# Statistics between eight stages from products and table guesses, and expert results scattered inside the loop

## The reference

```python
x = x + _layernorm(_L0_attn_ref(_layernorm(x, axis=-1), ...), axis=-1)
...
x = x + _layernorm(_L3_ffn_ref(_layernorm(x, axis=-1), ...), axis=-1)
```

## Time and profile before

| | |
|---|---|
| median of 3 runs | 3815.13 us (3812.38 to 3821.34) |
| the profiled execution | 3813.27 us, its span 3812.0 us |
| busy in the span | TensorE 82%, VectorE 71%, ScalarE 59%, POOL 38% |
| stages end at | titan 262, split 531, linear 596, moe1 821, mamba 1166, gqa 1610, mla 1887, layer0 3812 us |

### The profile page before, as it was taken

The page is one execution under the profiler, slowest core; times in us unless marked ns, Lnnn a source line. Parts: engine busy times, 40 slices in busy tenths (PEclk is TensorE's granted clock), DMA queues, the critical chain, the costliest instruction groups (busy, mean ns, idle before and its releaser), DMA issues.

```text
span 3812.0 us, 102302 instructions
## 1 busy us (share of the span) xinstructions
PE 3127.3 (82%) x41325; PEld 2030.5 (53%) x41325; DVE 2696.3 (71%) x7087; ACT 2240.9 (59%) x5623; POOL 1455.2 (38%) x1443
## 2 busy tenths in 40 slices
PE   6878865727776879877579999999999999999997
PEld 5544544712333546545446666666666666666665
DVE  6466567546796555579787777777777777777773
ACT  4234442426553332258757777777777777777775
POOL 0110010335672000000066665656665666565651
PEclk9989987958987989989899999999999999999997
DMA  1000001810000000000001111111111111211110
GB/s 54 1 5 1 2 12 51 230 65 0 0 1 5 2 1 1 30 1 2 30 21 29 25 28 54 28 26 27 56 26 27 55 28 25 58 24 29 24 29 22
DMA packets 50454, 108.05 MB, mean 28 GB/s; under 512 B 7376, under 2 KB 17488, under 8 KB 48192
## 3 DMA queue, kind: packets, MB, share of 16 engines
q1 hardware_dynamic: 47456, 96.33, 9.3%
q0 software_dynamic: 2528, 5.18, 0.7%
HBM read 52.27 MB, written 5.18 MB: 15 GB/s over the span
## 4 chain that ended last, share of the span: by engine, by line
PE 45%; DVE 23%; ACT 14%; issue 5%; POOL 3%; DMA 1%; POOLq 0%; SPq 0%; DVEq 0%; ACTq 0%
PE psum L3164 5%; PE psum L3221 5%; PE psum L401 5%; PE psum L3204 4%; PE psum L3114 4%; PE psum L406 4%; PE psum L1145 4%; PE psum L1998 3%; DVE scratch L3376 2%; PE psum L1199 2%; DVE xnT L3526 2%; DVE xnT L3413 2%; POOL scratch L2609 1%; ACT L3280 1%; PE psum L3189 1%
## 5 line engine op out<-in xcount | busy, mean ns | idle before, releaser
L3566 POOL TENSOR_TENSOR scratch<-scratch 128x512 f32<-128x512 f32 x384 | 488.1, 1271 | 409.9 <-DVE scratch L3379 409.7
L406 PEld LDWEIGHTS psum<-table,scratch 128*128 128x128 f32 (+1 forms) x2284 | 281.5, 144 | 293.6 <-issue 234.7
L3221 PE MATMUL psum<-weights,scratch 128*128 128x512 f32 x768 | 413.2, 620 | 14.5 <-ACT y L3316 14.1
L406 PE MATMUL psum<-table,scratch 128*128 128x128 f32 (+1 forms) x2284 | 367.4, 282 | 44.7 <-DVE scratch L2699 11.8
L3579 POOL TENSOR_TENSOR scratch<-scratch,xnT 128x512 f32<-128x512 f32 x384 | 401.4, 1045 | 0.0
L3376 DVE TENSOR_TENSOR scratch<-psum,xnT 128x512 f32<-128x512 f32 x384 | 264.3, 688 | 146.0 <-PE psum L3221 139.2
L3350 ACT COPY scratch<-psum 128x512 f32<-128x512 f32 x384 | 225.5, 587 | 157.1 <-PE psum L406 151.0
L3316 ACT ACTIVATE y<-psum 128x512 f32<-128x512 f32 x384 | 230.8, 601 | 104.3 <-DVE scratch L3379 91.1
L3526 DVE TENSOR_REDUCE xnT<-y 128x8 f32<-128x512 f32 x384 | 253.9, 661 | 1.4
L1145 PE MATMUL psum<-scratch 32*128 32x256 f32 (+1 forms) x2560 | 179.1, 392 | 69.2 <-DVE weights L1406 20.4
L3501 DVE TENSOR_REDUCE scratch<-psum 128x4 f32<-128x256 f32 x384 | 161.1, 419 | 72.8 <-PE psum L3189 71.2
(11 more groups left out here) (538 smaller groups left out, 7725.6 us busy)
## 6 DMA issues: line engine op xcount, KB each, us to landing
scratch<-scratch SPq DMA_DIRECT2D x96, 256.0 KB, 3.2
scratch<-experts_dram SPq DMA_DIRECT2D x47, 384.0 KB, 4.3
scratch<-scratch SPq DMA_DIRECT2D x96, 128.0 KB, 3.2
weights<-layer_dram SPq DMA_DIRECT2D x6, 1357.0 KB, 9.6
weights<-layer_dram SPq DMA_DIRECT2D x6, 1356.5 KB, 7.0
scratch<-scratch SPq DMA_DIRECT2D x96, 64.0 KB, 2.9
weights<-gqa_dram SPq DMA_DIRECT2D x2, 1738.5 KB, 8.7
results_dram<-scratch SPq DMA_DIRECT2D x11, 256.0 KB, 4.0
```

The costliest lines, as they stand in the source:

```text
L406: return self.nc.tensor.transpose(out, src, self.c("ident")[0:k, 0:k])
L3221: mm(raw_bank(a), window(m)[:, i * P:i * P + P], weight(m, "wqkv")[:, at:at + 512], start=True, stop=True).then_inc(S("rows_made").up(), 1)
L3566: gtt(out, out, sines, ALU.add).then_inc(S("rope_sum").up(), 1)
```

## The change

1. **Statistics of the sum without the sum.** `dve_see_tiles` makes, beside `bn_stats` of y, the product x*y with its sum over the row (`accum_out`). From it `between` gets the variance of x + norm(y) by arithmetic on 128x16 values, before the sum exists. The mean of y is not taken off; the shifts are added up in `shifts` and subtracted in the last stage (`dve_set_shift`). `dve_sum` adds scaled y to x tile by tile, three tiles while a guess is awaited, the rest among the rows of xn.
2. **Guessed roots.** ScalarE guesses 1/sqrt with Ln and Exp (`act_guess`) and VectorE makes one round (`dve_exact`) instead of the seed and three rounds. The table that holds both functions is loaded at the start of `between`.
3. **Rows.** ScalarE writes three of four tiles of xn, VectorE one (two and two before the first stage).
4. **moe1.** POOL scatters each tile's results (to the token's row in `results`, or to rows aside for empty places) in the loop, 20 tiles behind the gathers, all transfers of POOL in one order over four semaphores; gathers run up to 10 tiles ahead. After the loop SP waits for the last four and loads both results of each group with plain transfers on the semaphores of the weights.

```diff
+def shifts(M):
+    return M.stats[:, 480:480 + TILES]
+def products(M):
+    return M.stats[:, 384:384 + TILES]
+def dve_see_tiles(M, first, n):
     nc, dve = M.nc, M.dve
     st, _ = stats_room(M, Y_ROOM, TILES)
+    M.wait_loaded(dve, "x")
     for t in range(first, first + n):
         nc.vector.bn_stats(st[:, t, :], M.y[:, t, :]).then_inc(dve.link(), 1)
+        dve.at_least(dve.chain, M.multiplied)
+        nc.vector.scalar_tensor_tensor(M.stats[:, 512:512 + DIM], M.y[:, t, :], 1.0, M.x[:, t, :], ALU.mult,
+                                       ALU.mult, accum_out=products(M)[:, t:t + 1]).then_inc(dve.link(), 1)
+        M.multiplied = dve.chain.made
     M.seen = first + n
+def dve_see(M, first, n, signal, k):
+    M.dve.wait_ge(signal, k)
+    dve_see_tiles(M, first, n)
+def act_guess(M, src, out):
+    act = M.act
+    act.wait_ge(M.sig("var_out"), M.guesses)
+    M.nc.scalar.activation(out, src, ACT.Ln).then_inc(act.link(), 1)
+    act.settle()
+    M.nc.scalar.activation(out, out, ACT.Exp, scale=-0.5).then_inc(M.sig("guessed").up(), 1)
+    M.guesses += 1
+def dve_exact(M, x, y, t):
+    nc, dve = M.nc, M.dve
+    dve.wait_ge(M.sig("guessed"), M.guesses - 1)
+    nc.vector.tensor_tensor(t, x, y, ALU.mult).then_inc(dve.link(), 1)
+    dve.settle()
+    nc.vector.scalar_tensor_tensor(t, t, -0.5, y, ALU.mult, ALU.mult).then_inc(dve.link(), 1)
+    dve.settle()
+    nc.vector.scalar_tensor_tensor(y, t, 1.5, y, ALU.add, ALU.mult).then_inc(dve.link(), 1)
+def dve_sum(M, t):
+    _, r = stats_room(M, Y_ROOM, TILES)
+    M.nc.vector.scalar_tensor_tensor(M.x[:, t, :], M.y[:, t, :], r[:, 5, t:t + 1], M.x[:, t, :], ALU.mult, ALU.add).then_inc(
+        M.sig("x_sum").up(), 1)
+def between(M, added, root):
     nc, dve, act, S = M.nc, M.dve, M.act, M.sig
+    tt, ts, stt = nc.vector.tensor_tensor, nc.vector.tensor_scalar, nc.vector.scalar_tensor_tensor
+    _, x = stats_room(M, X_ROOM, TILES)
+    tiles = lambda src: [src[:, t, :] for t in range(TILES)]
+    early = 0
+    nc.scalar.preload_act_table_set("natural_log_exp_and_others")
     M.wait_ended(dve)
     M.wait_ended(act)
+    if added:
+        _, y = stats_room(M, Y_ROOM, TILES)
+        dve_see_tiles(M, M.seen, TILES - M.seen)
+        dve_moments(M, tiles(M.y), TILES, Y_ROOM, done=S("var_out"), seen=TILES)
+        act_guess(M, y[:, 4, :], y[:, 5, :])
+        dve.wait_ge(S("var_out"), 0)
+        stt(y[:, 1, :], x[:, 0, :], -2.0, y[:, 0, :], ALU.mult, ALU.mult).then_inc(dve.link(), 1)
+        dve.settle()
+        stt(y[:, 2, :], products(M), 2.0 / DIM, y[:, 1, :], ALU.mult, ALU.add).then_inc(dve.link(), 1)
+        dve_exact(M, y[:, 4, :], y[:, 5, :], y[:, 3, :])
+        dve.settle()
+        stt(y[:, 3, :], y[:, 5, :], -EPS, y[:, 2, :], ALU.mult, ALU.add).then_inc(dve.link(), 1)
+        tt(y[:, 1, :], y[:, 0, :], y[:, 5, :], ALU.mult).then_inc(dve.link(), 1)
+        dve.settle()
+        tt(y[:, 3, :], y[:, 3, :], y[:, 5, :], ALU.mult).then_inc(dve.link(), 1)
+        dve.settle()
+        stt(x[:, 4, :], y[:, 3, :], 1.0, x[:, 4, :], ALU.add, ALU.add).then_inc(S("var_out").up(), 1)
+        early = 3
+        tt(x[:, 0, :], x[:, 0, :], y[:, 1, :], ALU.add).then_inc(dve.link(), 1)
+        tt(shifts(M), shifts(M), y[:, 1, :], ALU.add).then_inc(dve.link(), 1)
+        for t in range(early):
+            dve_sum(M, t)
+        dve.wait_ge(S("var_out"), 1)
+    else:
+        nc.vector.memset(shifts(M), 0.0).then_inc(dve.link(), 1)
+        dve_moments(M, tiles(M.x), TILES, X_ROOM, done=S("var_out"), seen=TILES)
+        dve.wait_ge(S("var_out"), 0)
+    act_guess(M, x[:, 4, :], x[:, 5, :])
+    dve_exact(M, x[:, 4, :], x[:, 5, :], x[:, 3, :])
+    dve.settle()
+    stt(x[:, 1, :], x[:, 0, :], -1.0, x[:, 5, :], ALU.mult, ALU.mult).then_inc(S("x_scaled").up(), 1)
+    scale, shift, out, done = x[:, 5, :], x[:, 1, :], M.xn, S("x_scaled")
     if root:
+        square, inverse = x[:, 2, :], x[:, 3, :]
         room, scale2, shift2 = (M.stats[:, 400 + 32 * i:416 + 32 * i] for i in range(3))
+        stt(square, x[:, 4, :], -EPS, x[:, 5, :], ALU.add, ALU.mult).then_inc(dve.link(), 1)
+        dve.settle()
+        tt(square, square, x[:, 5, :], ALU.mult).then_inc(dve.link(), 1)
+        dve.settle()
+        ts(square, square, EPS, None, ALU.add).then_inc(S("var_out").up(), 1)
+        dve.wait_ge(S("var_out"), M.guesses)
+        act_guess(M, square, inverse)
+        if added:
+            for t in range(early, early + 3):
+                dve_sum(M, t)
+            early += 3
+        dve_exact(M, square, inverse, room)
+        dve.settle()
+        tt(scale2, x[:, 5, :], inverse, ALU.mult).then_inc(dve.link(), 1)
+        tt(shift2, x[:, 1, :], inverse, ALU.mult).then_inc(S("x_rooted").up(), 1)
         scale, shift, out, done = scale2, shift2, M.y, S("x_rooted")
+    M.by_dve = 1 if added else 2
     dve.wait_ge(done, 0)
     act.wait_ge(done, 0)
     for g in range(GROUPS):
+        for k in range(4):
+            t = 4 * g + k
+            if added and t >= early:
+                dve_sum(M, t)
+            if k >= M.by_dve:
+                if added:
+                    act.wait_ge(S("x_sum"), t)
+                nc.scalar.activation(out[:, t, :], M.x[:, t, :], ACT.Identity, bias=shift[:, t:t + 1],
+                                     scale=scale[:, t:t + 1]).then_inc(S("xn_act").up(), 1)
+        for t in range(4 * g, 4 * g + M.by_dve):
+            if added:
+                dve.wait_ge(S("x_sum"), t)
+            ts(out[:, t, :], M.x[:, t, :], scale[:, t:t + 1], shift[:, t:t + 1], ALU.mult, ALU.add).then_inc(S("xn_dve").up(), 1)
     if root:
+        for t in range(TILES):
+            nc.scalar.activation(M.xn[:, t, :], M.x[:, t, :], ACT.Identity, bias=x[:, 1, t:t + 1],
+                                 scale=x[:, 5, t:t + 1]).then_inc(S("xn_kept").up(), 1)
+    M.seen = 0
...
 def wait_xn(M, engine, g):
-    engine.wait_ge(M.sig("xn_act" if g % 2 else "xn_dve"), 4 * (g // 2) + 3)
+    engine.wait_ge(M.sig("xn_dve"), M.by_dve * (g + 1) - 1)
+    engine.wait_ge(M.sig("xn_act"), (4 - M.by_dve) * (g + 1) - 1)
...
-    PAIRS, CHUNK, MOVES, AHEAD = 2 * TILES, 8, 3, 6
+    PAIRS, CHUNK, MOVES, AHEAD, BEHIND = 2 * TILES, 8, 4, 10, 20
...
-                pe.wait_ge(S(f"rows_moved{j % MOVES}"), j // MOVES)
+                wait_moved(pe, nth_fetch(j))
...
+        stt(R.aside, c("iota", SORTED), float(P), c("token", 1).broadcast_to([P, SORTED]), ALU.mult, ALU.add).then_inc(dve.link(), 1)
+        dve.settle()
+        ts(R.aside, R.aside, float(2 * TOKENS), None, ALU.add).then_inc(dve.link(), 1)
+        stt(R.goal, M.bank(7)[:, 0:SORTED], 0.5, R.aside, ALU.is_lt, ALU.mult).then_inc(dve.link(), 1)
+        dve.settle()
+        stt(R.goal, M.bank(7)[:, 0:SORTED], -1.0, R.goal, ALU.add, ALU.add).then_inc(dve.link(), 1)
+        dve.settle()
+        nc.vector.tensor_copy(R.goal_of.bitcast(I32), R.goal).then_inc(S("tables").up(), 1)
...
-            for n in range(8 * g, 8 * g + 8):
-                dve.wait_ge(S(move(SORTED + n)), (SORTED + n) // MOVES)
+            dve.wait_ge(S(f"fetch_moved{g}"), fetched(g) + 1)
...
+    def nth_fetch(j):
+        return j + max(0, j - BEHIND)
+    def nth_put(j):
+        return BEHIND + 1 + 2 * j if j + BEHIND < SORTED else SORTED + j
+    def wait_moved(engine, n):
+        if n >= 0:
+            engine.wait_ge(S(f"rows_moved{n % MOVES}"), n // MOVES)
+    def moved(n):
+        return S(f"rows_moved{n % MOVES}").up()
+    def fetched(i):
+        return len(range(i, SORTED, RING))
-        for j in range(SORTED):
-            pool.wait_ge(S(move(j)), j // MOVES - 1)
-            pool.wait_ge(S("turned"), j - AHEAD)
-            at = bass.IndirectOffsetOnAxis(ap=R.token_of[:, j:j + 1].bitcast(U32), axis=0)
-            nc.gpsimd.indirect_dma_start(xs[:, j, :], None, M.dram["tokens"], at).then_inc(S(move(j)).up(), 16)
-        pool.wait_ge(S("y_moved"), GROUPS + NORMS - 1)
-        for n in range(PAIRS):
-            i, k = divmod(n, 2)
-            pool.wait_ge(S(move(SORTED + n)), (SORTED + n) // MOVES - 1)
-            at = bass.IndirectOffsetOnAxis(ap=R.place_of[:, k * TILES + i:k * TILES + i + 1].bitcast(U32), axis=0)
-            nc.gpsimd.indirect_dma_start(back[:, k, i, :], None, M.dram["results"], at).then_inc(S(move(SORTED + n)).up(), 16)
-    def store(q):
-        sp.wait_ge(S("mixed"), q)
-        t = slice(tiles_of(q)[0], tiles_of(q)[-1] + 1)
-        nc.sync.dma_start(by_rows(M.dram["results"])[:, t, :], xs[:, t, :]).then_inc(S("y_moved").up(), 16)
+        for n in range(SORTED + BEHIND):
+            j = n
+            if j < SORTED:
+                wait_moved(pool, nth_fetch(j) - MOVES)
+                pool.wait_ge(S("turned"), j - AHEAD)
+                at = bass.IndirectOffsetOnAxis(ap=R.token_of[:, j:j + 1].bitcast(U32), axis=0)
+                nc.gpsimd.indirect_dma_start(xs[:, j, :], None, M.dram["tokens"], at).then_inc(moved(nth_fetch(j)), 16)
+            j = n - BEHIND
```

(28 more changed lines are left out.)

98 lines of the change are left out of this document (25 added, 73 removed).

## The result

The changed kernel takes 3797.95 us (3795.32 to 3801.48, five runs) against 3815.13: ratio 0.9952, interval 0.9939 to 0.9965. That is 17 us of the 66 that were forecast. The profiled execution has a span of 3794.2 at a mean clock of 0.937.

| segment, us | before | after | difference | forecast, same cut | missing |
|---|---|---|---|---|---|
| start | 15.57 | 14.91 | -0.7 | -2.7 | 2.0 |
| titan | 261.57 | 253.50 | -8.1 | -6.1 | -2.0 |
| split | 270.15 | 261.37 | -8.8 | -8.0 | -0.8 |
| linear | 64.49 | 67.46 | +3.0 | -5.0 | 8.0 |
| moe1 | 223.65 | 228.95 | +5.3 | -28.5 | 33.8 |

The account below looks back on a forecast made before the run. No engine is full: eight stages each have their own limit, and VectorE works alone between them. Terms of -84.2 and +18.4 gave -65.8 on 3813.3, 3747.5; with 1.9 for the median, 3749 us, range 3736 to 3768.

Parts of the forecast that it names:

- The boundary: Between two stages: xn's first row starts 4.5 us after the first operation on y, against 14.28 before.
- the change doesn't do what it says: Rival at the boundaries: Ln and Exp from different tables, reloaded at each of 14 guesses; +36, 3785; chance 0.03.
- The products' own price: Product with accumulation beside bn_stats, 16 tiles a stage: 0.25 us each, 69 on the path, 17.0 lost.
- The rival at half rate: VectorE's new operations read two f32 SBUF tiles at half rate, in products and boundaries; 3774; chance 0.07.
- mamba 4 and half of 12: In mamba, 4 products and half of 12 more lie on the path, at 0.25 us each.
- 8.5: Time saved at each of the seven boundaries between stages, in us; 59.5 together.
- POOL's prelude for layer0: Before layer0, POOL's prelude waits for VectorE's later last row of xn; 0.9 us of the gain lost.
- the next stage's start held by something that this trace hides: Sign listed among those that would show the forecast wrong, at the start of a stage; no size given.
- moe1, the transfers: In moe1: 27 gather-scatter pairs at 2.66 us, 20 scatters alone at 1.3, then four groups at 4.66.
- Gain 20: In moe1: scattering in the loop and plain loads afterwards save 20 us, bounds 6 and 22.
- 47 scatters in the loop cost only POOL's own time: In moe1's loop: scatters were priced through POOL's 94 transfer issues, 1.33 us apart with a landing of 5.
- POOL's turns are the bound: Rival in moe1: landings of 5.9 make a pair take 3.1, the scatters end 14 later; 3763; chance 0.14.

Follow-up runs that it names:

- e4: Changed kernel with mamba's twelve loop products of y and x taken after the loop; 3792.27 us, ratio 0.9936.
- e6: Changed kernel with one POOL subtraction made early, in split, and repeated bias copies for linear written as one operation; 3810.27 us, ratio 0.9971.
- e13: The changed kernel executed again, nothing altered; 3772.54 us, ratio 0.9889.
- e17: The changed kernel executed a third time, nothing altered; 3771.61 us, ratio 0.9888.
- e1: Changed kernel with the new code between stages but the moe1 stage as before the change; 3795.07 us, ratio 0.9949.
- e8: The edits of e1, e4 and e6 together, against the kernel before; 3781.13 us, ratio 0.9901.
- e11: e8 with POOL's start in linear held back until the second group of xn's rows is there; 3777.76 us, ratio 0.9891.
- e5: e1 with a second, unread gather beside each gather of moe1's loop (added work); 3849.64 us, one run.
- e7: Changed kernel with scatters 34 tiles behind the gathers instead of 20; 3809.11 us, ratio 0.9973.
- e9: Changed kernel with gathers at most 3 tiles ahead instead of 10; 3806.20 us, ratio 0.9974.
- e10: Changed kernel with POOL clearing 512 columns and waiting after each scatter of the loop's mixed part (added work); 3794.19 us, one run.
- e12: Changed kernel with e10's pauses, e4's late products and e11's held-back POOL start in linear; 3769.23 us, ratio 0.9881.
- e18: Changed kernel with e4's late products and e11's held-back POOL start in linear, no pauses, second execution; 3757.28 us, ratio 0.9843.
- e16: The kernel before the change executed again; 3815.01 us, one run.

## Why the prediction was right and wrong

- **The boundary: right.** The first row comes 4.50 to 4.76 after the start in five boundaries against a forecast of 4.5, and 6.72 with the second root against 6.6; ScalarE's 12 rows take 5.04 against 4.75; the last eviction ends at 604.13, 11.4 against 11.1. From gqa to mla it comes at 6.05, for before had 15.84 there too: two steps of VectorE on 16 columns take 1.8 beside a memset of POOL's in both traces, and the table load that the forecast charged with 0.3 hides beside them. The rival "the change doesn't do what it says" is out: each boundary has one load of the table, at its start, and none between Ln and Exp. titan, split and mla shrank by 8.1, 8.8 and 5.9.
- **The products' own price: 0.20, not 0.25.** `bn_stats` and product follow each other at 0.405, `bn_stats` alone at 0.205; the read of the accumulator lies under the next. On 16 products that is 0.8 less than forecast, in titan and in gqa. The rival at half rate is out too: a product alone takes 0.27, no more than other operations of 128 columns. The Trainium skill (Vector Engine (DVE) Microarchitecture Reference, Points that are easy to get wrong) says that such an operation runs at half throughput; the measurement differs, and it decides.
- **Mamba: the step "mamba 4 and half of 12" at 0.25 failed**, by 12. Ten products were priced at 2.5 us; beside POOL's multiplies they took up to 2.21 each, and all 16 took 19.4. e4 shows it: 12.8 less when they wait. Before's trace had the sign, which I did not look for: the same kind of operation on two operands in SBUF takes 1.20 at 909.07 and 2.15 at 1063.03, with a multiply of POOL's from 1061.75 to 1064.09:

```profile
909.07 1.20 DVE L2604 SCALAR_TENSOR_TENSOR scratch<-scratch 128x1024 f32<-128x1024 f32 x1
...
1061.75 2.34 POOL L2609 TENSOR_TENSOR scratch<-scratch 128x1024 f32<-128x1024 f32 x1 [2.47 <-PE psum L2469]
...
1063.03 2.15 DVE L2604 SCALAR_TENSOR_TENSOR scratch<-scratch 128x1024 f32<-128x1024 f32 x1
```

  The Trainium skill (SBUF — State Buffer, Who interferes with whom) has the rule: a VectorE instruction with two inputs in SBUF contends with a GpSimd instruction that reads SBUF, and the ports that they share are an exclusive lock. The traces agree (2.21 for 0.27, 1.04 for 0.17).
- **Linear: the saving was counted at "8.5" in each boundary although work of POOL was hidden in this one.** The forecast weighed POOL's prelude for layer0 alone (0.9) and named the rest only as "the next stage's start held by something that this trace hides". The tables take 24 us (524.03 to 548.0), and as long a chain, with a gap of 7.60 in it, was in before's trace. The segment is short by 8.0, of which e6's edit gives back 5 to 6.
- **moe1, the transfers: right where nothing is late.** Pairs of issues come every 2.57 (forecast 2.66), the last scatter starts 121.6 after the first gather (121), the groups are 4.4 apart (4.66). In e13, e17 the segment is 202.4 and 201.5; against e1's 220.5 the new stage gives 18 to 19, where the forecast says "Gain 20". That compares two conditions: e1's trace lacks records, though its rows of issues in the loop have at most five transfers and it has no long wait; e8 and e11, with the same stage, have 225.6 and 226.4.
- **moe1, the signals: the step that 47 scatters in the loop cost only POOL's own time failed in the first measurement.** There 127 us went into a loop of 95, since most late signals of TensorE reached ScalarE only when POOL's row of issues had ended. Shown: in such executions the longest gaps stand behind the longest rows (e5, e7, e9), the waits are shorter with pauses (e10, one execution), and whole runs go without them (e12 to e18). Open: what puts an execution into that condition, and whether the recording has a part in it. It was not the chip, and not the kernel alone.
- **moe1, the router's matmuls: a gain eaten by the clock.** Windows from xn's first row to the end of the router's matmuls, before and then after (columns as above):

```profile
611.77:621.75 9.98, 7.91 (x48) 7.46 (x48) 3.52 (x10) 4.36 (x10) 0.00 (x0) 0.67 0.37 105
```

```profile
597.24:611.30 14.06, 11.32 (x48) 9.76 (x48) 5.73 (x19) 6.02 (x14) 0.00 (x0) 0.50 0.27 76
```

  The granted clock is 0.50 throughout after, its lower level of 1.2 GHz, where it rose to the upper before; 32 small matmuls take 6.98 instead of 4.26. TensorE's idle time before the boundary's transposes was 8.99 after and 17.37 before, so it isn't the longer pause that goes with the slower start; e1 and e13 show the 6.98 too, e16 has 4.33. It goes on behind the router: after, the clock is at 0.50 until 628.08 and again from 645.15, and 32 matmuls of 128x512 take 16.15 instead of 14.00, 64 of 128x47 8.77 instead of 7.75. With evictions that end 1.4 later, this makes the 7.2 by which the gathers begin later behind xn. The forecast held 1.3 of them; the other 5.9 are what moe1 is short by in the repeats. It had no term for the clock; why the clock rises in the one and not in the other was not tried.
- **What is left.** By the repeats (mean of e13 and e17 less that of before and e16, by the spans) the change is worth 41.7 and not 66: mamba is short by 14, linear by 8.5, moe1 by 6, layer0 and the start by 2 each and mla by 1, while titan is better by 4 and gqa by 5. gqa's 5 goes with the clock, for which the forecast had no term, and is luck: its segment takes 431.9 us with 53 of them at the lower level (the changed kernel), 432.7 with 61 (e13, e9), 435.2 with 67 (e4, e18) and 438.5 with 73 (e5, e6), and before had 441.6 with 73. layer0 is 1910 in before and 1912 to 1917 in all with the new boundaries. What moves the slow stretches was not tried.

In the rivals' terms: "POOL's turns are the bound" is out (pairs every 2.57 in e13, not 3.1), and slow landings didn't come (2.3 for the last scatter). Its price was also summed too low: 74 transfers at 0.22 more each are 16 us and not 14. The range, 3736 to 3768, missed both 3797.95 and the repeats' 3772, because it held no case for late signals, for a stage that hides work of POOL, or for two engines at SBUF at once.

## What to carry to other kernels

Before a stretch in which one engine works alone is shortened, list what the others do under it: here it hid most of 24 us of POOL's, and some 5 of them came into the open. An operation added to VectorE is priced by what POOL does beside it (0.27 or 2.21), for which the same operation elsewhere in the old trace is the place to look. And repeat a measurement before explaining a few tenths of a per cent: one kernel gave ratios 0.9952 and 0.9889 on two occasions, with intervals apart.
